# Product slabs of a deformable sampling summed by 32x32 tile matmuls, with GpSimd making three of the ten slabs

## The chip, the cores and the metric

The kernel runs on one core of a Trainium2 chip. The metric is the device time of one execution in microseconds; the median of three runs of the kernel before is 114.21 us (113.84 to 116.41). Engines are named as in the profile: PE is TensorE's matmul, PEld its weight load, DVE VectorE, ACT ScalarE, POOL GpSimd, SP SyncE with the DMA queue. A difference of about 2% is what is called a difference here.

## What is computed

A batch of four images, 64 channels, 16 by 16 points, goes through three layers: a deformable convolution block, a gated attention over the 256 tokens, and a mixture of eight experts of which two are used. The change lies in the first, in its sampling:

```python
def _bilinear_sample(img, grid):                 # img (8, 18, 18), grid (256, 9, 2)
    ...
    return gather(y0, x0) * w00 + gather(y0, x1) * w01 + gather(y1, x0) * w10 + gather(y1, x1) * w11

def _dcnv3_core(x, offset, mask):                # 8 groups of 8 channels, 9 points each
    ...
    sampled = jax.vmap(_bilinear_sample)(xin, sgf)
    m = mask.reshape(B, H * W, G, P).transpose(0, 2, 1, 3).reshape(B * G, 1, H * W, P)
    out = (sampled * m).sum(-1)
    ...
def _forward(...):
    h = gelu(conv1x1(x)); u = h; h = dwconv5(h)
    attn = dcn(h)                                # v = h @ inproj; offsets and softmax masks; _dcnv3_core; @ outproj
    attn = _conv1x1(attn, conv_w, conv_b)
    return _conv1x1(u * attn, proj2_w, proj2_b) + shortcut
```

## The kernel before

Every engine's program is written out by hand, in a fixed order, with semaphores between them. The four images are handled as two halves of two (`BL = 2`, called `bl` below and "first" and "second image"; each is really a pair, one on partitions 0 to 63, one on 64 to 127). Tokens lie on partitions in sampling, four x positions beside each other in the free dimension (`VW = 256` columns).

Sampling avoids the gather. As long as offsets stay under one point, the nine sampling points of a token touch a window of 5 by 5 pixels. `v_win` holds that window (five rows `dy`, loaded by 20 DMAs from `v_padded`). The 25 weights of the window are summed on PE: VectorE makes `ym` (hat functions in y times the softmax weights `prob`) and then three `terms` per image (`window_terms`, jx = 0 and 1 on VectorE, the third on GpSimd in `side_terms`), and `window_weights` on PE adds them through matmuls with the identity into PSUM (15 matmuls of up to 288 columns, 30 records: a float32 matmul is recorded as two). `products(bl, dy)` on VectorE then multiplies one row of the window, five taps of 256 columns, by its weights, which it reads from PSUM. These five slices of 256 columns are a product slab; there are five slabs per image. GpSimd's `merge` adds slices 3 and 4 into 0 and 1, and `window_sum` on PE adds the three slices that are left into `bank(bl, 2)`, with the full identity as weights. `MERGED = 5, 4` says how many slabs GpSimd merges; the last is merged by VectorE (`merge_last`).

`mask_sums` and `inverse_sums` make the softmax denominators on VectorE. `normalise` multiplies the sum by them, `to_channels` transposes on PE (8 matmuls of 64x64), `samples` copies on ScalarE, `project` and `close_l0` end the layer, with `shortcut` adding the layer's input in front. `flags` finds out whether some offset was too large; `over` on ScalarE sums the excess, GpSimd reads the flag and would compute the sampling slowly (with these inputs it doesn't) and then sets `slow_done`, for which `to_channels` waits. `keep_warm` issues matmuls on zeros while PE would be idle.

Matmul instructions of PE all carry the line of the helper `mm` (L1080).

## Time and profile before

| | |
|---|---|
| runs | 113.84, 114.21, 116.41 us |
| profiled execution, span | 114.8 us (114.82 in the trace) |
| granted TensorE clock, mean | 0.940 |
| instructions recorded | 1623, of them PE 569 matmuls and 573 weight loads |
| longest piece of the chain | PE, 57.38 to 68.97 us, 62 records |

The profile is that of one execution. Positions are microseconds from the span's start. In a timeline or in the chain, one line can stand for several instructions of the same kind that follow each other (x16): its time then reaches from the first's start to the last's end. Starts of a matmul are measured, its end is modelled, so a matmul's own time overlaps the next one's. An "idle before" in brackets names what ended the wait. The granted clock is a share of 2.4 GHz.

### The profile page before, as it was taken

How to read it: one execution, taken by the hardware profiler on the slowest of the kernel's cores; microseconds unless marked ns; L12 is line 12 of the kernel's file. 1: busy time of each engine (PE TensorE's matmuls, PEld its weight loads, DVE VectorE, ACT ScalarE, POOL GpSimd, SP SyncE). 2: the span in 40 equal slices, each digit the busy share in tenths (PEclk: the TensorE clock that was granted, in tenths of full speed). 3: DMA queues.
4: the chain of work that ended last, by engine and by line, in shares of the span. 5: the costliest groups of instructions: out<-in, count | busy, mean ns of one | idle time of the engine just before them, and what ended most of it. 6: DMA issues, size and time to landing. Idle time of an engine off the chain costs nothing.

```text
span 114.8 us, 1623 instructions
## 1 busy us (share of the span) xinstructions
PE 101.9 (89%) x569; PEld 71.4 (62%) x573; DVE 76.2 (66%) x172; ACT 48.0 (42%) x106; POOL 41.4 (36%) x51
## 2 busy tenths in 40 slices
PE   5999910999999899999799999899899899999990
PEld 1578800677745559899477786557696558864340
DVE  0489921799520699999999923657940836947751
ACT  2299200343980896100000023487833994964000
POOL 7137999089400072815799800000000006200000
PEclk9999998559965699999999999999999999999999
DMA  2995000000013662650000000000000000000002
GB/s 57 406 331 233 0 0 0 0 0 0 6 46 79 206 201 78 201 173 34 0 0 3 0 0 0 0 6 0 0 0 0 0 6 3 0 3 0 0 0 91
DMA packets 3225, 6.20 MB, mean 54 GB/s; under 512 B 528, under 2 KB 1296, under 8 KB 3216
## 3 DMA queue, kind: packets, MB, share of 16 engines
q1 hardware_dynamic: 2784, 4.64, 12.7%
q10 hardware_dynamic: 432, 1.46, 3.6%
q8 instruction: 4, 0.07, 0.2%
q14 instruction: 5, 0.04, 0.1%
HBM read 5.16 MB, written 0.93 MB: 53 GB/s over the span
## 4 chain that ended last, share of the span: by engine, by line
PE 56%; DVE 14%; ACT 10%; issue 10%; POOL 8%; DVEq 0%; ACTq 0%
PE ps L1080 55%; POOL prod L459 6%; DVE prod L861 3%; DVE ym L832 2%; DVE terms L841 2%; ACT prod L682 2%; ACT prod L602 1%; ACT L727 1%; ACT L595 1%; POOL prod L494 1%; DVE lmax L816 1%; DVE smax L908 1%; DVE psum_p L846 1%; ACT prod L615 1%; ACT upad L593 1%
## 5 line engine op out<-in xcount | busy, mean ns | idle before, releaser
L1080 PE MATMUL ps<-prod,wts 128*128 128x256 f32 (+1 forms) x122 | 28.8, 403 | 7.3 <-POOL prod L459 5.5
L1080 PEld LDWEIGHTS ps<-prod,wts 128*128 128x128 f32 (+1 forms) x122 | 17.6, 177 | 15.3 <-POOL prod L459 5.9
L1080 PE MATMUL ps<-terms,wts 128*128 128x256 f32 (+3 forms) x104 | 20.5, 350 | 0.0
L1080 PEld LDWEIGHTS ps<-terms,wts 128*128 128x128 f32 x104 | 16.9, 190 | 2.6 <-issue 0.4
L459 POOL TENSOR_TENSOR prod<-prod 128x256 f32<-128x256 f32 x10 | 12.8, 1313 | 5.7 <-ACT prod L602 5.7
L861 DVE TENSOR_TENSOR prod<-v_win,ps 128x1280 f32<-128x1280 f32 x10 | 14.3, 1462 | 0.0
L494 POOL TENSOR_TENSOR prod<-prod 128x512 f32<-128x512 f32 x9 | 11.5, 1273 | 5.3 <-DVE prod L861 4.9
L566 POOL TENSOR_TENSOR terms<-terms 128x256 f32<-128x256 f32 x2 | 1.4, 724 | 28.8 <-DVE terms L958 28.7
L669 ACT ACTIVATE samp_t<-ps 128x256 f32<-128x256 f32 x2 | 1.3, 640 | 23.3 <-PE ps L1080 23.3
L485 POOL TENSOR_TENSOR terms<-ym,hat 128x864 f32<-128x864 f32 x2 | 5.8, 2888 | 13.1 <-DVE ym L832 13.1
L1080 PE MATMUL ps<-idle 128*128 128x512 bf16 x27 | 8.7, 462 | 1.4 <-DVE idle L744 1.3
L1080 PE MATMUL ps<-upad,terms 128*128 128x256 f32 x36 | 8.1, 382 | 0.0
L762 DVE SCALAR_TENSOR_TENSOR acc<-upad,wts,acc 128x256 f32<-128x256 f32 x20 | 8.0, 476 | 0.0
L1080 PEld LDWEIGHTS ps<-upad,terms 128*128 128x128 f32 x36 | 6.8, 188 | 1.2
L1080 PEld LDWEIGHTS ps<-idle 128*128 128x128 bf16 x31 | 3.2, 109 | 6.4 <-issue 2.6
L1070 DVE TENSOR_TENSOR prod<-prod,ps 128x512 f32<-128x512 f32 x8 | 5.4, 687 | 2.3 <-PE ps L1080 2.3
L738 ACT ACTIVATE prod<-ps,wts 128x512 f32<-128x512 f32 x8 | 5.2, 687 | 2.0 <-PE ps L1080 2.0
L841 DVE TENSOR_TENSOR terms<-ym,hat 128x864 f32<-128x864 f32 x4 | 5.9, 1508 | 0.1
L1080 PE MATMUL ps<-wts,x 64*64 64x216 f32 x32 | 5.5, 509 | 0.5 <-issue 0.5
L602 ACT ACTIVATE prod<-hpad,wts 128x256 f32<-128x256 f32 x4 | 1.7, 497 | 10.0 <-DVE hpad L790 10.0
L1080 PE MATMUL ps<-hpad,cen 128*128 128x256 f32 x12 | 5.0, 602 | 0.0
L1080 PEld LDWEIGHTS ps<-hpad,cen 128*128 128x128 f32 x12 | 3.8, 328 | 1.3 <-issue 0.4
(165 smaller groups left out, 156.6 us busy)
## 6 DMA issues: line engine op xcount, KB each, us to landing
v_win<-v_padded SPq DMA_DIRECT2D x20, 128.0 KB, 2.8
wts<-in_w ACTq DMA_DIRECT2D x1, 984.0 KB, 8.5
wts<-in_w SPq DMA_DIRECT2D x1, 640.0 KB, 8.1
v_padded<-s_v SPq DMA_DIRECT2D x1, 400.0 KB, 8.1
wts<-in_w ACTq DMA_DIRECT2D x1, 280.0 KB, 4.1
x_in<-in_x SPq DMA_DIRECT2D x1, 256.0 KB, 3.2
v_padded<-v_tok SPq DMA_DIRECT2D x4, 64.0 KB, 2.0
out<-res SPq DMA_DIRECT2D x2, 128.0 KB, 1.7
```

Of the source, the lines that this page charges most:

```text
L459: g.tensor_tensor(part[:, bl, :], scaled[:, bl, 0, :] if k == 1 else part[:, bl, :], scaled[:, bl, k, :], ALU.add).then_inc(step[bl], 1)
L485: g.tensor_tensor(terms[:, bl, K3 - 1, :, :], ym[:, bl, :, :], hat[:, bl, K3 - 1, 0, :].unsqueeze(1).broadcast_to([P, K3, NPT * XG]), ALU. ...
L494: g.tensor_tensor(into, into, prod[:, bl, dy, 3:5, :], ALU.add).then_inc(merge_done, 1)
L602: a.activation(grid(scaled[:, bl, k, :]), padded[:, bl, y0:y0 + H, x0:x0 + W], ACT.Copy, scale=w(weights, first + k, first + k + 1)).then_ ...
L682: a.activation(pr[:, bl, bh * IT + it, :], bank(bl, bh)[:, it * HW:(it + 1) * HW], ACT.Exp, bias=nbias[:, bl, it, bh:bh + 1], accum_out=pr ...
L738: a.activation(h_act[:, bl, ep, :], hid_bank(bl, ep), ACT.Gelu, bias=w("b1", ep, ep + 1)).then_inc(gelu_done, 1)
L762: v.scalar_tensor_tensor(out=to, in0=src, scalar=w(weights, k, k + 1), in1=to, op0=ALU.mult, op1=ALU.add).then_inc(step[bl], 1)
L832: v.tensor_tensor(ym[:, bl, :, :], hat[:, bl, :, 1, :], prob[:, bl, :].unsqueeze(1).broadcast_to([P, K3, NPT * XG]), ALU.mult).then_inc(ym ...
L841: v.tensor_tensor(terms[:, bl, jx, :, :], ym[:, bl, :, :], hat[:, bl, jx, 0, :].unsqueeze(1).broadcast_to([P, K3, NPT * XG]), ALU.mult).th ...
L861: v.tensor_tensor(prod[:, bl, dy, :, :].rearrange("p d (x c) -> p d x c", c=GC), win, a5_rows(bl, dy, dy + 1)[:, 0].unsqueeze(3).broadcast ...
L1070: v.tensor_tensor(h_cmb[:, bl, ep % 2, :], h_act[:, bl, ep, :], bank(bl, 2), ALU.mult).then_inc(hcmb_done, 1)
L1080: return nc.tensor.matmul(out_, lhsT, rhs, start=start, stop=stop, skip_group_check=True)
```

## The change

- The three terms of an image are all made by VectorE, in the order jx = 1, 0, 2, image after image; GpSimd's `side_terms`, its merges, `merge_last` and the reduces `mask_sums` are gone.
- The softmax denominators are summed on PE: nine matmuls per image within `window_weights`, after the first of the three terms, into columns behind the weights (`mask_sum`). The reciprocal is taken image by image from PSUM.
- GpSimd makes three product slabs, (0, 4), (1, 3) and (1, 4). It cannot read PSUM, so ScalarE copies their window weights to SBUF (`copy_a5`).
- `window_sum` sums the 25 slices of 256 columns of an image by 100 matmuls of 32x32 (identity `ident4`): row group `r` of partitions goes to its own PSUM bank, slice `n` to the partitions of group `n % 4`. The four banks then hold four by four partial sums. ScalarE (for the second image ScalarE and VectorE) copies them to `by_slab`, and `sum_slabs` adds the four column groups by four matmuls that place every row group where it belongs. The banks 6 and 7 serve both images, so `window_sum(1, 0)` waits for the copies of the first.
- `shortcut` moves from in front of the second image's weights into `close_l0`; `to_channels` writes to bank 3, `t0` to bank 2. `sq`, `lnv`, `rstd`, `xn` become parts of one tensor `ln_room`, in which the copies also lie. `window_sum(0, 0)` waits for both images' flags.

```diff
-MERGED = 5, 4
+TILE = 32
+TG = P // TILE
+POOLED = (4,), (3, 4)
+        def slab_bank(bl, r):
+            return ps[:, ((2, 3, 6, 7), (0, 1, 6, 7))[bl][r], :]
 (GpSimd)
+            def products(bl, dy):
+                pool.wait_ge(v_windowed[bl], 16 * BH * K5)
+                pool.wait_ge(a5_copied, bl + 1)
...
+                g.tensor_tensor(prod[:, bl, dy, :, :].rearrange("p d (x c) -> p d x c", c=GC), win,
+                                weights.unsqueeze(3).broadcast_to([P, K5, XG, GC]),
+                                ALU.mult).then_inc(pool_prod_done, 1)
 (ScalarE)
+            def copy_a5(bl):
+                act.wait_ge(a5_done, bl + 1)
+            def copy_slabs(bl, half_):
+                act.wait_ge(slabs_done, bl + 1)
+                if bl:
+                    act.wait_ge(sum_done, bl)
 (TensorE)
+                    if jx == order[0]:
+                        for q in range(NPT):
+                            mm(mask_sum(bl), w("ident"), prob[:, bl, q * XG:(q + 1) * XG], False, False)
             def window_sum(bl, dy):
                 if dy == 0:
-                    pe.wait_ge(far_set, bl + 1)
+                    pe.wait_ge(ident4_set, 1)
+                    pe.wait_ge(far_set, BL)
+                    if bl:
+                        pe.wait_ge(prod_done, K5 - len(POOLED[0]))
+                        pe.wait_ge(slabs_act, 2)
...
+                for dx in range(K5):
+                    n = dy * K5 + dx
+                    o0, o1 = row_group(n % TG)
+                    for r in range(TG):
+                        p0, p1_ = row_group(r)
+                        last = mm(slab_bank(bl, r)[o0:o1, 0:VW], ident4[p0:p1_, :],
+                                  prod[p0:p1_, bl, dy, dx, :], n < TG, n >= K5 * K5 - TG)
+            def sum_slabs(bl):
+                pe.wait_ge(slabs_act, (2, 3)[bl])
+                if bl:
+                    pe.wait_ge(slabs_dve, 1)
+                for r in range(TG):
+                    o0, o1 = row_group(r)
+                    last = mm(bank(bl, 2)[o0:o1, 0:VW], ident4[:, :], by_slab[:, r, :])
+                last.then_inc(sum_done, 1)
             def close_l0(bl):
+                pe.wait_ge(xb_ready, 1)
+                mm(bank(bl, 3)[:, 0:HW], w("center"), xb[:, bl, :], True, False)
```

Where instructions stand now. On PE, before, from the last two terms of the first image's weights (jx = 0) to the second image's first term and then from the sums on (`terms,wts` are window weights, `over_sum` the flags, `xb` the shortcut):

```order
L1080 MATMUL ps<-terms,wts 128x3x96
L1080 MATMUL ps<-terms,wts 128x2x96
L1080 MATMUL ps<-terms,wts 128x96 x2
L1080 MATMUL ps<-terms,wts 128x2x96
L1080 MATMUL ps<-wts,over_sum 1x1 x2
L1080 MATMUL ps<-xb,wts 128x256 x2
L1080 MATMUL ps<-terms,wts 128x3x96
```

The same place with the change:

```order
L1112 MATMUL ps<-prob,wts 128x32 x9
L1112 MATMUL ps<-terms,wts 128x3x96
L1112 MATMUL ps<-terms,wts 128x2x96
L1112 MATMUL ps<-terms,wts 128x96 x2
L1112 MATMUL ps<-terms,wts 128x2x96
```

The nine `prob` matmuls stand behind the first term of each image, and the shortcut is no longer between the flags and the second image's weights.

PE from the second image's weights to the last close, before:

```order
L1080 MATMUL ps<-prod,wts 128x256 x24
L1080 MATMUL ps<-wts,samp 64x64 x8
L1080 MATMUL ps<-prod,wts 128x256 x6
L1080 MATMUL ps<-samp_t,w_oc 128x256
L1080 MATMUL ps<-wts,samp 64x64 x8
L1080 MATMUL ps<-zu,w2c 128x256
L1080 MATMUL ps<-zu,wts 128x256
L1080 MATMUL ps<-samp_t,w_oc 128x256
```

And with the change:

```order
L1112 MATMUL ps<-prod,ident 32x256 x120
L1112 MATMUL ps<-ln_room,ident 32x256 x4
L1112 MATMUL ps<-prod,ident 32x256 x20
L1112 MATMUL ps<-wts,samp 64x64 x8
L1112 MATMUL ps<-prod,ident 32x256 x20
L1112 MATMUL ps<-samp_t,w_oc 128x256
L1112 MATMUL ps<-prod,ident 32x256 x40
L1112 MATMUL ps<-xb,wts 128x256
L1112 MATMUL ps<-zu,w2c 128x256
L1112 MATMUL ps<-zu,wts 128x256
L1112 MATMUL ps<-ln_room,ident 32x256 x4
L1112 MATMUL ps<-wts,samp 64x64 x8
```

30 matmuls became 200 and eight more; `to_channels(0)`, `project(0)` and `close_l0(0)` lie between the second image's slabs.

ScalarE with the change, behind the exponential of the second image, waits named (L684 is `over`, L691 `copy_a5`, L699 `copy_slabs`, L705 `samples`):

```order
L684 ACTIVATE s_pos,over_sum<-o_abs,wts 128x576 [waits abs_done]
L691 ACTIVATE ln_room<-ps 128x160 [waits a5_done]
L684 ACTIVATE s_pos,over_sum<-o_abs,wts 128x576 [waits abs_done]
L691 ACTIVATE ln_room<-ps 128x320 [waits a5_done]
L699 ACTIVATE ln_room<-ps 128x512 [waits slabs_done] x2
L705 ACTIVATE samp_t<-ps 128x4x64 [waits sT_done]
L699 ACTIVATE ln_room<-ps 128x512 [waits sum_done,slabs_done]
```

Before, the two `over` instructions followed each other directly, and then came the two `samples`. The second `over`, for which the flags on PE wait, is now behind a copy that waits for the first image's weights.

## Rows read from the trace of the kernel before

**Rows 1.** The page: busy time of each engine, share of the span, instructions.
```profile
PE 101.9 (89%) x569; PEld 71.4 (62%) x573; DVE 76.2 (66%) x172; ACT 48.0 (42%) x106; POOL 41.4 (36%) x51
```
**Rows 2.** The chain of work in order of time: start us, us, what.
```profile
57.38 11.59 PE ps L1080 x62
...
68.99 0.43 DVE samp L879
```
**Rows 3.** Timeline of PE, weights to slabs: start us, us, engine, line, operation, tiles.
```profile
42.56 4.91 PE L1080 MATMUL ps<-terms,wts 128*128 128x288 f32 x30
47.40 0.24 PE L1080 MATMUL ps<-wts,over_sum 128*1 128x1 f32 x4
47.57 1.13 PE L1080 MATMUL ps<-xb,wts 128*128 128x256 f32 x4
48.53 4.91 PE L1080 MATMUL ps<-terms,wts 128*128 128x288 f32 x30
53.28 1.89 PE L1080 MATMUL ps<-prod,wts 128*128 128x256 f32 x8
```
**Rows 4.** Timeline of DVE products; then two groups of GpSimd adds (busy us, mean ns).
```profile
55.96 7.05 DVE L861 TENSOR_TENSOR prod<-v_win,ps 128x1280 f32<-128x1280 f32 x5
...
L494 POOL TENSOR_TENSOR prod<-prod 128x512 f32<-128x512 f32 x9 | 11.5, 1273 | 5.3 <-DVE prod L861 4.9
...
L566 POOL TENSOR_TENSOR terms<-terms 128x256 f32<-128x256 f32 x2 | 1.4, 724 | 28.8 <-DVE terms L958 28.7
```
**Rows 5.** Timeline of softmax and terms: DVE, GpSimd, and ScalarE's `over`.
```profile
38.13 0.66 DVE L816 TENSOR_REDUCE lmax<-lg 128x32 f32<-128x288 f32 x1 [4.47 <-ACT lg L637]
...
39.88 1.06 DVE L832 TENSOR_TENSOR ym<-hat,prob 128x864 f32<-128x864 f32 x1 [0.24 <-ACT prob L655]
40.97 1.06 DVE L841 TENSOR_TENSOR terms<-ym,hat 128x864 f32<-128x864 f32 x1
...
44.62 0.76 ACT L663 ACTIVATE s_pos<-o_abs,wts 128x576 f32<-128x576 f32 x1
45.28 0.19 ACT L663 ACTIVATION_READ_ACCUMULATOR s_pos<-o_abs,wts 128x1 f32 x1
...
46.34 3.85 DVE L841 TENSOR_TENSOR terms<-ym,hat 128x864 f32<-128x864 f32 x2
46.38 2.88 POOL L485 TENSOR_TENSOR terms<-ym,hat 128x864 f32<-128x864 f32 x1 [2.47 <-DVE ym L832]
```
**Rows 6.** Timeline of PE's weight loads at the router (16 columns each).
```profile
94.83 0.52 PEld L1080 LDWEIGHTS ps<-wts,terms 128*128 128x128 f32 x4 [0.26 <-DVE terms L958]
```
**Rows 7.** Groups of ScalarE's copies out of PSUM: busy us, mean ns.
```profile
L688 ACT ACTIVATE prod<-ps 128x512 f32<-128x512 f32 x2 | 1.2, 597 | 1.4 <-PE ps L1080 1.4
L676 ACT ACTIVATE terms<-ps 128x256 f32<-128x256 f32 x2 | 0.8, 390 | 0.0
```
**Rows 8.** Timeline of 64x64 matmuls; the second row is 74.77 to 74.81 alone.
```profile
74.78 1.09 PE L1080 MATMUL ps<-terms 64*64 64x256 f32 x16
...
74.78 0.45 PE L1080 MATMUL ps<-terms 64*64 64x256 f32 x4
...
65.48 0.54 PEld L1080 LDWEIGHTS ps<-wts,samp 64*64 64x64 f32 x16 [0.33 <-issue]
```
**Rows 9.** Timeline of the tail, ScalarE and PE.
```profile
68.79 0.59 PE L1080 MATMUL ps<-samp_t,w_oc 128*128 128x256 f32 x2
...
70.19 0.63 ACT L669 ACTIVATE samp_t<-ps 128x256 f32<-128x256 f32 x1 [3.33 <-PE ps L1080]
...
71.05 0.59 PE L1080 MATMUL ps<-samp_t,w_oc 128*128 128x256 f32 x2
...
73.08 0.59 PE L1080 MATMUL ps<-zu,wts 128*128 128x256 f32 x2
```
**Rows 10.** Stretches: us, busy PE, PEld, DVE, ACT, POOL, clock, DMA share, GB/s.
```profile
31.00:33.00 2.00, 2.00 (x27) 1.55 (x25) 0.42 (x1) 1.97 (x4) 0.00 (x0) 0.92 0.00 0
33.00:39.00 6.00, 5.53 (x29) 2.68 (x28) 1.26 (x3) 2.31 (x5) 0.00 (x0) 0.50 0.41 118
```

More of the change, by code:

```diff
@@ L118, in conv_attn_moe @@
         acc3 = sb("acc3", [P, BL, HW])
-        sq = sb("sq", [P, BL, HW])
-        lnv = sb("lnv", [P, BL, HW])
-        rstd = sb("rstd", [P, BL, HW])
-        xn = sb("xn", [P, BL, HW])
+        ln_room = sb("ln_room", [P, 4 * BL, HW])
+        sq, lnv, rstd, xn = (ln_room[:, i * BL:(i + 1) * BL, :] for i in range(4))
         x1 = sb("x1", [P, BL, HW])
@@ L479, in _ @@
                     left = b2_rest[:, i, :]
-            def side_terms(bl):
-                pool.wait_ge(ym_done, bl + 1)
-                pool.wait_ge(hats_done, 2 * bl + 2)
-                g.tensor_tensor(terms[:, bl, K3 - 1, :, :], ym[:, bl, :, :],
-                                hat[:, bl, K3 - 1, 0, :].unsqueeze(1).broadcast_to([P, K3, NPT * XG]),
-                                ALU.mult).then_inc(side_terms_done, 1)
-            def merge(bl):
-                for dy in range(MERGED[bl]):
-                    pool.wait_ge(prod_done, K5 * bl + dy + 1)
-                    into = prod[:, bl, dy, 0:2, :]
-                    g.tensor_tensor(into, into, prod[:, bl, dy, 3:5, :], ALU.add).then_inc(merge_done, 1)
+            def products(bl, dy):
+                pool.wait_ge(v_windowed[bl], 16 * BH * K5)
+                pool.wait_ge(a5_copied, bl + 1)
+                row = v_win[:, bl, dy, 0:VW]
+                win = bass.AP(row.tensor, row.offset, [list(row.ap[0]), [C, K5], [GC, XG], [1, GC]])
+                weights = a5_rows_sb[:, bl, dy - AR, :].rearrange("p (d x) -> p d x", d=K5)
+                g.tensor_tensor(prod[:, bl, dy, :, :].rearrange("p d (x c) -> p d x c", c=GC), win,
+                                weights.unsqueeze(3).broadcast_to([P, K5, XG, GC]),
+                                ALU.mult).then_inc(pool_prod_done, 1)
+            for dy in POOLED[0]:
+                products(0, dy)
+            products(1, POOLED[1][0])
             for bl in range(BL):
-                side_terms(bl)
-            for bl in range(BL):
-                merge(bl)
+                if bl:
+                    for dy in POOLED[1][1:]:
+                        products(1, dy)
                 pool.wait_ge(far_set, bl + 1)
@@ L706, in _ @@
             over(0)
+            copy_a5(0)
             over(1)
+            copy_a5(1)
+            copy_slabs(0, 1)
+            copy_slabs(0, 0)
             samples(0)
+            copy_slabs(1, 0)
             samples(1)
@@ L958, in normed3 @@
                 v.tensor_tensor(x2[:, bl, :], bank(bl, 0)[:, 0:HW], rstd3[:, bl, :], ALU.mult).then_inc(x2_done, 1)
-            softmax(0)
-            masked_hats(0)
-            window_terms(0, 1)
-            softmax(1)
-            window_terms(0, 0)
-            masked_hats(1)
-            window_terms(1, 1)
-            window_terms(1, 0)
-            mask_sums(0)
-            products(0, 0)
-            flags(0)
-            mask_sums(1)
-            products(0, 1)
-            inverse_sums()
-            products(0, 2)
+            for bl in range(BL):
+                softmax(bl)
+                masked_hats(bl)
+                for jx in (1, 0, 2):
+                    window_terms(bl, jx)
+            flags(0)
+            inverse_sums(0)
+            products(0, 0)
             flags(1)
-            products(0, 3)
-            products(0, 4)
+            for dy in range(1, K5):
+                if dy not in POOLED[0]:
+                    products(0, dy)
+            inverse_sums(1)
             products(1, 0)
             products(1, 1)
+            normalise(0)
             products(1, 2)
-            normalise(0)
-            products(1, 3)
-            products(1, 4)
-            merge_last()
+            gate_u(0)
+            copy_slabs(1, 1)
             normalise(1)
-            gate_u(0)
             gate_u(1)
@@ L1303, in _ @@
             flags(1)
-            for bl in range(BL):
-                shortcut(bl)
             window_weights(1)
@@ L1309, in _ @@
             window_sum(1, 0)
+            sum_slabs(0)
             window_sum(1, 1)
+            to_channels(0)
             window_sum(1, 2)
-            to_channels(0)
+            project(0)
             window_sum(1, 3)
             window_sum(1, 4)
-            project(0)
+            close_l0(0)
+            sum_slabs(1)
             to_channels(1)
-            close_l0(0)
             project(1)
```

82 lines of the change are left out of this document (44 added, 38 removed).

## Prediction

> **What bounds the kernel now.** I read the page's summary first [rows 1]: PE is busy 89% of the span, VectorE 66%. The chain in order of time [rows 2] says where this change acts: 62 PE records from 57.38 to 68.97 are its longest piece, and the second image's `normalise` at 68.99 ends it. The timeline of PE [rows 3] gives the positions that all sums below start from. The first image's window weights (30 records) start at 42.56, the next work at 47.40, so they take 4.84; the second image's start at 48.53, and the first slab is fed at 53.28. After that PE has 60 full-array records of 256 columns, 0.213 apart ((1.89 - 0.4) / 7 [rows 3]), 12.8 us, and reaches `project(0)` at 68.79 [rows 9], because VectorE hands over a product every 1.41 us and GpSimd merges one in 1.27 [rows 4]. So two things alternate as the bound: PE up to 53.3, then the trio of VectorE, GpSimd and PE at nearly equal pace. The change gives the second stretch a new shape and makes the first one longer.
>
> **The front: window weights.** All terms now come from VectorE: three of 1.06 behind each `ym`. From the first at 40.97 that puts the end of the first image's third at 44.15; from softmax's start to `ym` 1.75 (38.13 to 39.88), `ym` 1.06 and three more terms: 50.1 [rows 5]. VectorE took the second image's two terms in 3.85 instead of 2.1, because GpSimd's 2.88 instruction lay beside them [rows 5]; without that neighbour the third term costs VectorE nothing: 50.1 is also when it was free before. PE needs the terms later than they come.
> New on PE are the mask sums, nine matmuls (18 records) per image of 32 columns with the full 128-column `ident` as weights. The nearest row is the router, 16 columns behind full weights: four weight loads in 0.52, each lasting 0.19, so (0.52 - 0.19) / 3 = 0.11 a record [rows 6]. 18 x 0.11 = 1.98 an image. First image: 42.56 + 4.84 + 1.98 = 49.4.
> Then ScalarE stands in the way: `over(1)` is now behind `copy_a5(0)`, which waits for those weights. From PE being free to ScalarE's start 0.2 (68.79 to the `normalise` at 68.99 [rows 2, 9]); copy of 160 columns about 0.3 (256 take 0.39 [rows 7]); `over(1)` 0.85 (44.62 to 45.47 [rows 5]). So PE's `flags(1)` waits until 50.8, and behind it in PE's queue are all second weights: 50.9 + 4.84 + 1.98 = **57.7**. Before, that was 53.2. PE idles 1.4 there, and the first slab is summed 4.5 us later, although VectorE has made its four products by 56.3 (from 50.5, behind flag and reciprocal, 1.41 each) and GpSimd its one.
>
> **The slabs.** A slab is now 20 matmuls of 32x32, 40 records of 256 columns. No row shows a 32x32 tile. What rows show is 64x64: 16 records of 256 columns in 1.09, four of them beginning within 0.04 [rows 8]; one after another they would need 3.4. Four tiles really run at once. With sixteen, 40 x 0.213 / 16 = 0.53 a slab; that is the lower bound. Upper bound: the eight 64x64 matmuls of 64 columns, 16 loads in 0.54 of which the last lasts 0.13, 0.41 / 15 = 0.027, at 40 records 1.1 a slab; were no tile to run beside another, 8.5, which the same rows exclude. I call the cost s and take s = 0.60: the four-tile row is the nearest, and it loses only at its end.
> The Trainium skill, "TensorE: Matmul & The Clock Gate", section "Measured speedup vs the span model", gives 10.6 times for sixteen tiles, not 16. By it, s = 20 x 0.427 / 10.6 = 0.81, and the sum below would be 1.9 us longer. Its number is for one isolated pack; it is the first rival below.
>
> **The sum from 57.7.** Five slabs of the first image in one go (5s). Then `window_sum(1, 0)` must wait for ScalarE to empty the same banks: 0.2 + two copies of 512 columns at 0.60 [rows 7] = 1.4. One slab (s). `sum_slabs(0)`, eight records on four column tiles, 0.45, semaphore 0.2. `normalise` 0.42, and only behind it product (1, 2), 1.47 with its gap. Slab (1, 1) and `to_channels(0)` hide under these. Slab (1, 2) (s), `project(0)` 0.43, two slabs (2s); `close_l0(0)`, now with the shortcut, three matmuls 1.3, which hides the two copies of the last slabs (0.2 + 0.6); `sum_slabs(1)` 0.45, 0.2. Constants 6.35, so `normalise(1)` starts at 57.7 + 6.35 + 9s = 64.05 + 9s, which is 9s - 4.94 later than before. At 0.60 that is 69.45; before it was 68.99 [rows 2]: **+0.46**.
> GpSimd: three products. From 256 to 512 elements its add goes from 0.72 to 1.27, and the 864 ones, without the wait for VectorE's 1.06, last 49.26 - 47.40 = 1.86 [rows 4, 5]; on that line 1280 elements cost about 2.7, at worst 2.888 x 1280 / 864 = 4.3. The second image's two start at 58.3 and end at 63.7 (at worst 66.9). PE asks for the last one s + 1.95 before the end of the sum, at 62.1 + 8s = 66.9. Cost nothing, even at worst. GpSimd's far test (`slow_done`) comes behind the first of them, at 61.1, before `to_channels(0)` asks at 63.8. Before, products on VectorE beside merges on GpSimd lasted the usual 1.41 [rows 4], so these two forms don't block each other.
> VectorE loses two reduces, a merge and three products, and gains two terms and a copy; idle from 56.3 to 58.3, it is no longer a bound, so this is worth nothing by itself.
> The tail: `close_l0(0)` no longer stands before `project(1)`, but ScalarE's `samp_t` copy is in front of it anyway (70.82 against 71.05 [rows 9]); the shortcut, once in front of the weights (0.96 between 47.57 and 48.53, counted above), now adds 0.43 to the stretch `project(1)`, variance, two idle matmuls, `close_l0(1)`. Start of the last `proj2`: 69.45 + 0.43 + 0.7 + 0.7 + 0.1 = 71.4 for `project(1)`, five matmuls of 0.43 behind it, 73.5; before 73.08. So the tail gives back nothing and adds nothing: total **+0.5**. Profiled span 114.82, so 115.3; the median of the runs shown, 114.21, is 0.6 under the profiled execution, so **114.7 us**.
>
> **Rivals.** A difference of about 2% (2.3 us) is what a measurement of this kernel can tell from no change.
> *Each pack pays its end* (14%). The 16 records of the four-tile row took 1.09, where four rounds of 0.213 are 0.85; if every slab pays that 0.24, s = 0.77 and the time is 114.2 + 9 x 0.77 - 4.94 = 116.2. For it: every slab but the first image's starts after a wait. Against: five slabs run back to back.
> *The small matmuls are limited by issue* (15%), the slower side. A slab has 80 instructions where it had 12. If a pair never takes less than the 0.027 of the short 64x64 row, s = 1.1 and the time is 114.2 + 9.9 - 4.9 = 119.2. It decides from s = 0.80 upward. Against it: in that row the columns themselves (64 on two tiles) fill the time, and in the other one eight instructions begin within 0.04 [rows 8]. The Trainium skill, "Runtime: NRT & Kernel Launch", section "Instruction fetch mechanics", speaks of about 20 sequencer cycles an instruction; by it s would be 1.33 and the time some 2 us above this rival. The 0.04 speaks against that, but only for a short run of instructions.
> *The clock falls* (12%). The granted clock was 0.50, its lower level of 1.2 GHz, from 33 to 39 after a stretch of small 64x64 matmuls in which PE counted as busy nearly all the time [rows 10]. The same after these sparse stretches: six microseconds at half clock, somewhat over half of them PE-bound, +3.5: 118.2.
> *Weights that stay* (7%), the faster side: if the repeated `ident` loads cost 0.03 instead of 0.11, 36 x 0.08 = 2.9 comes off the front: 111.8. The router row and the 96-column pieces in the 4.84 speak against it.
> That the work isn't moved at all can't be: order and data are fixed in the program.
>
> **Numbers.** Forecast 50%, others as above, 2% for what I haven't seen. Within 2%: the forecast and half of the first rival, 0.57. Slower: 0.15 + 0.12 + 0.07 + 0.02 = 0.36. Faster 0.07. The range leaves out most of the faster case and the top of the issue case: 112.8 to 118.9. The forecast's own range is 113.9 to 115.6 (s from 0.53 to 0.65, 0.4 either way for copies and semaphores).
>
> **What would show it.** Second weights end on PE near 57.7 with a gap of 1.4 before them; mask sums 2.0 an image; five slabs in 2.7 to 3.2; a gap of 1.4 behind them; `normalise(1)` at 69.5; clock at its upper level throughout; GpSimd products 2.7. I am wrong if five slabs take over 4, or if the weights come before 56.

## The result, and the profile after

The changed kernel takes 119.09 us (median of four runs, 118.03 to 121.41), the kernel before, measured beside it, 115.29 us (113.84 to 116.41): a ratio of 1.041 with a 95% interval of 1.028 to 1.055. It is slower; the forecast was 114.7 with a range up to 118.9.

Executions of every kernel here come in a faster and a slower kind, so ratios and their intervals compare the faster ones alone, while medians and the lowest and highest time take all. The first window weights start near 40 us in some profiles and near 43 us in others, in which the granted clock stands at a half for longer before them. So dates are compared from the start of the first window weights, which I call W. The profiled execution of the changed kernel has W at 43.04; before it was 42.56 [rows 3], so 0.48 of every later date is not the change's.

The page of the changed kernel, to be read against [rows 1, 4]: the summary, and three groups of section 5 (line, engine, operation, tiles, count, then busy us and mean ns of one, then idle before).

```profile
PE 103.4 (87%) x961; PEld 71.3 (60%) x965; DVE 70.4 (59%) x171; ACT 50.3 (42%) x111; POOL 31.6 (26%) x43
...
L510 POOL TENSOR_TENSOR prod<-v_win,ln_room 128x1280 f32<-128x1280 f32 x3 | 7.2, 2417 | 25.8 <-ACT ln_room L691 25.8
...
L1112 PE MATMUL ps<-prod,ident 32*32 32x256 f32 x400 | 10.0, 385 | 1.5 <-ACT ln_room L699 1.4
```

VectorE lost 5.8 us of work and GpSimd 9.8; PE gained 1.5 although its matmuls became small. So the engines that shared the second stretch are relieved, and PE alone paces it. The mean of 385 ns for a tile's record of 256 columns is not the price of one, since up to sixteen lie over each other; what they cost together has to be read from the timeline.

The timeline of PE in the changed kernel, from the first window weights to the second image's turn to channels (start us, us, engine, line, operation, tiles, records, and in brackets the idle time before with what ended it), against [rows 3, 9]:

```profile
43.04 1.75 PE L1112 MATMUL ps<-terms,wts 128*128 128x288 f32 x10
44.62 2.09 PE L1112 MATMUL ps<-prob,wts 128*128 128x32 f32 x18
...
51.10 0.19 PE L1112 MATMUL ps<-wts,over_sum 128*1 128x1 f32 x2 [1.03 <-ACT s_pos L684]
...
58.18 4.08 PE L1112 MATMUL ps<-prod,ident 32*32 32x256 f32 x200
63.64 1.35 PE L1112 MATMUL ps<-prod,ident 32*32 32x256 f32 x40 [1.38 <-ACT ln_room L699]
64.91 0.64 PE L1112 MATMUL ps<-ln_room,ident 128*32 128x256 f32 x8
65.48 1.29 PE L1112 MATMUL ps<-prod,ident 32*32 32x256 f32 x40
66.71 0.68 PE L1112 MATMUL ps<-wts,samp 64*64 64x64 f32 x16
67.49 1.29 PE L1112 MATMUL ps<-prod,ident 32*32 32x256 f32 x40
68.72 0.70 PE L1112 MATMUL ps<-samp_t,w_oc 128*128 128x256 f32 x2
69.35 1.99 PE L1112 MATMUL ps<-prod,ident 32*32 32x256 f32 x80
71.27 0.70 PE L1112 MATMUL ps<-xb,wts 128*128 128x256 f32 x2
```

The chain of work of the same stretch (start us, us, what), where [rows 2] had one piece of 62 PE records:

```profile
51.10 11.17 PE ps L1112 x226
62.27 0.02 issue
62.30 1.09 ACT ln_room L699 x2
63.39 0.24 issue
63.64 1.96 PE ps L1112 x47
65.60 0.02 issue
65.62 0.07 DVE samp L919
65.69 0.28 issue
65.96 1.49 DVE prod L907
67.45 0.04 issue
67.49 5.95 PE ps L1112 x129
73.44 0.02 issue
73.47 0.44 DVE samp L919
```

`normalise(1)` starts at 73.47, 30.43 after W; before it was 68.99 - 42.56 = 26.43. The 4.0 us between them are the whole loss: from there to the end of the span it is 45.8 or 45.9 in both (119.34 - 73.47, 114.82 - 68.99). They split at the first slab on PE: it starts 15.14 after W (58.18 - 43.04) where it was 10.72 (53.28 - 42.56 [rows 3]), 4.4 later, and from there to `normalise(1)` it is 15.29 where it was 15.71, 0.4 less. So the new summing is no slower than the old one. It was to win back 4.0 of what the front costs (15.71 - 11.75 by the forecast) and won back 0.4. The chain is PE nearly throughout; the only other links are two copies of ScalarE and one `normalise` with a product behind it.

### The profile page after: what moved, and what is told of

The parts are those of the page before. It is cut to its first block, busy times and chain, and to the rows that moved or that the text cites. A ratio compares the mean times of both kernels' runs of the same rounds, so it can differ in the third digit from the quotient of the medians.

```text
span 119.3 us, 2412 instructions
## 1 busy us (share of the span) xinstructions
PE 103.4 (87%) x961; PEld 71.3 (60%) x965; DVE 70.4 (59%) x171; ACT 50.3 (42%) x111; POOL 31.6 (26%) x43
## 4 chain that ended last, share of the span: by engine, by line
PE 69%; ACT 11%; POOL 6%; DVE 6%; issue 5%; ACTq 0%; DVEq 0%
PE ps L1112 69%; POOL prod L481 6%; ACT prod L718 2%; DVE prod L907 1%; ACT prod L623 1%; ACT L768 1%; ACT L616 1%; DVE smax L948 1%; ACT ln_room L699 1%; ACT upad L614 1%; ACT terms L643 1%; ACT terms L641 1%; ACT prod L636 1%; ACT s_pos L684 1%; ACT samp_t L705 1%
## 5 line engine op out<-in xcount | busy, mean ns | idle before, releaser
L1112 PE MATMUL ps<-terms,wts 128*128 128x256 f32 (+3 forms) x104 | 21.1, 352 | 0.0
L1112 PE MATMUL ps<-prod,wts 128*64 128x256 f32 (+1 forms) x62 | 14.3, 410 | 6.6 <-POOL prod L481 5.5
L510 POOL TENSOR_TENSOR prod<-v_win,ln_room 128x1280 f32<-128x1280 f32 x3 | 7.2, 2417 | 25.8 <-ACT ln_room L691 25.8
L1112 PEld LDWEIGHTS ps<-prod,wts 128*64 128x64 f32 (+1 forms) x62 | 7.0, 165 | 11.1 <-POOL prod L481 5.9
L1112 PE MATMUL ps<-prod,ident 32*32 32x256 f32 x400 | 10.0, 385 | 1.5 <-ACT ln_room L699 1.4
L907 DVE TENSOR_TENSOR prod<-v_win,ps 128x1280 f32<-128x1280 f32 x7 | 10.0, 1458 | 0.0
L1112 PEld LDWEIGHTS ps<-prod,ident 32*32 32x32 f32 x400 | 5.9, 103 | 4.7 <-issue 3.0
L691 ACT ACTIVATE ln_room<-ps 128x160 f32<-128x160 f32 (+1 forms) x2 | 0.7, 372 | 10.6 <-PE ps L1112 10.6
```

The source lines that it names most:

```text
L510: g.tensor_tensor(prod[:, bl, dy, :, :].rearrange("p d (x c) -> p d x c", c=GC), win, weights.unsqueeze(3).broadcast_to([P, K5, XG, GC]), ...
L907: v.tensor_tensor(prod[:, bl, dy, :, :].rearrange("p d (x c) -> p d x c", c=GC), win, a5_rows(bl, dy, dy + 1)[:, 0].unsqueeze(3).broadcast ...
L1112: return nc.tensor.matmul(out_, lhsT, rhs, start=start, stop=stop, skip_group_check=True)
```

## Experiments

Two kinds of question were open: why nine slabs cost 8.4 us on this path where 5.4 had been forecast, and what the other parts of the change (mask sums on PE, the order of `over`, GpSimd's slabs) are worth. In what follows a *turn* is four slices of 256 columns: four row groups times four column groups, each of the sixteen tiles used once, 16 matmuls, 32 records. By columns alone a turn lasts 2 x 0.213 = 0.427 us.

### Half the columns

```diff
-                        last = mm(slab_bank(bl, r)[o0:o1, 0:VW], ident4[p0:p1_, :],
-                                  prod[p0:p1_, bl, dy, dx, :], ...)
+                    wide = VW if n < TG else VW // 2
+                        last = mm(slab_bank(bl, r)[o0:o1, 0:wide], ident4[p0:p1_, :],
+                                  prod[p0:p1_, bl, dy, dx, 0:wide], ...)
```

> The changed kernel, but all slab matmuls except the first sixteen of each image stream 128 of the 256 columns (half of the sampling's sum is left out in those columns). It tells apart what sets the pace of the 200 records of the first image, which began within 3.70 us (58.18 to 61.88). Theory 1, issue: a pair of weight load and matmul cannot be fed faster than one per about 17 ns, so the 200 records still take 3.3 to 3.7 us. Theory 2, columns and tiles: the pace is that of the columns, 0.213 for 256, so the 168 shortened records run at about half and the stretch falls to 2.0 to 2.2 us. The single slabs of the second image (1.23 us each until PE is free): theory 1 about 1.2, theory 2 about 0.8.

Timeline of PE in this kernel:

```profile
54.75 3.02 PE L1112 MATMUL ps<-prod,ident 32*32 32x256 f32 x200
...
60.80 0.87 PE L1112 MATMUL ps<-prod,ident 32*32 32x128 f32 x40
61.60 0.68 PE L1112 MATMUL ps<-wts,samp 64*64 64x64 f32 x16
```

The first copy of the partial sums starts at 57.80, so the burst of five slabs takes 3.05 where it took 4.12 (62.30 - 58.18). A slab by itself went from 1.23 to 0.80 (61.60 - 60.80), two turns of 0.213 less. The burst, with 21 of its 25 slices halved, lost 1.07, five times 0.213; six of its seven turns hold halved slices. So columns count nearly in full, and neither theory holds alone: pure issue would have left the burst nearly as it was, pure columns would have made it 2.1.

The starts of single records, read in the trace one by one, say what lies above the columns. Behind the first turn of the changed kernel's burst, a group of 34 records starts every 0.645 us (at 58.83, 59.47, 60.12, 60.77, 61.41), with one pause of 0.16 in each. With half the columns the group comes every 0.43 with a pause of 0.04. A tile's two passes are 0.427 and 0.213, so both lie 0.22 above them. For a turn of 32 records that makes 0.61 and 0.41, some 0.18 above the columns in either case.

### Four slices of the second image's slabs

```diff
-                for dx in range(K5):
-                    n = dy * K5 + dx
+                taps_used = (K5, K5 - 1)[bl]
+                for dx in range(taps_used):
+                    n = dy * taps_used + dx
```

The sum of image 1 leaves out one of five slices of each slab here.

> The changed kernel with the fifth slice (dx = 4) of each of the second image's slabs left out, so that a slab standing alone is 16 matmuls, one for every tile. Theory A, second turn: five slices on four column groups need some tiles twice, 2 x 0.427, and then PE waits for the end of the last, 0.38, before it changes its tile shape; 1.24 in all. Without the fifth slice it is 0.43 + 0.38 = 0.81, so slab (1, 2) falls from 1.23 to 0.8 and slab (1, 0) from 1.27 to about 0.85. Theory B, issue: the cost follows the number of instructions, 1.23 x 4/5 = 0.98.

Timeline of PE in this kernel, three slabs that stand alone and the last two in one run, with what follows each:

```profile
60.51 0.96 PE L1112 MATMUL ps<-prod,ident 32*32 32x256 f32 x32 [1.38 <-ACT ln_room L699]
61.41 0.64 PE L1112 MATMUL ps<-ln_room,ident 128*32 128x256 f32 x8
61.98 0.73 PE L1112 MATMUL ps<-prod,ident 32*32 32x256 f32 x32
62.64 0.68 PE L1112 MATMUL ps<-wts,samp 64*64 64x64 f32 x16
63.99 0.73 PE L1112 MATMUL ps<-prod,ident 32*32 32x256 f32 x32 [0.67 <-DVE prod L907]
64.64 0.70 PE L1112 MATMUL ps<-samp_t,w_oc 128*128 128x256 f32 x2
65.27 1.50 PE L1112 MATMUL ps<-prod,ident 32*32 32x256 f32 x64
66.70 0.70 PE L1112 MATMUL ps<-xb,wts 128*128 128x256 f32 x2
```

Slabs (1, 1) and (1, 2) of four slices take 0.66 (62.64 - 61.98) and 0.65, one of five took 1.23. The first slab, which starts behind a wait for ScalarE, takes 0.90 where it took 1.27. So the fifth slice costs 0.4 to 0.6, as much as up to four others: it opens a second turn. Theory B's 0.98 is out; theory A had the turn right and its 0.8 somewhat too high. A second turn that is filled costs more still, as the last two slabs show (66.70 - 65.27). All runs of slices that were measured with 256 columns, from the first record's start to what follows on PE (for the 25, to the first copy):

| slices in a run | turns | their columns, us | measured, us |
|---|---|---|---|
| 4 | 1 | 0.43 | 0.65, 0.66, behind a wait 0.90 |
| 5 | 2 | 0.85 | 1.23, behind a wait 1.27 |
| 8 | 2 | 0.85 | 1.43 |
| 10 | 3 | 1.28 | 1.92 |
| 20 | 5 | 2.13 | 3.58, 4.06, 4.26 (three kernels further down) |
| 25 | 7 | 2.99 | 4.12 |

Whole turns of columns are a lower bound that every run keeps; 0.2 to 0.6 us come on top in the short ones, 1.1 in the burst, 1.5 and more at 20 slices. The simplest rule, 0.65 for the first turn and 0.58 for each one more, fits 4, 5 and 25 slices, and is short by 0.20 at 8, by 0.11 at 10 and by 0.6 or more at 20.

### Another order of the same matmuls

```diff
-                for dx in range(K5):
-                    for r in range(TG):
+                for n0 in range(0, K5 * K5, TG):
+                    for r in range(TG):
+                        for n in range(n0, min(n0 + TG, K5 * K5)):
```

> The burst of image 0 in another order: of four products at a time the four of one row group one after the other, then those of the next row group, where the changed kernel has the four row groups of one product and then the next product. The same 100 matmuls on the same tiles. Theory A (each turn of all sixteen tiles costs its columns, 0.427 us, and about 0.16 us for issuing its 32 pairs of records, in whatever order): the 200 records to the first copy of partial sums take 4.1 us again. Theory B (the order makes the tiles wait for one another): 3.4 us, or well over 4.5 where this order is the worse one.

The burst starts at 58.77, the first copy at 63.21: 4.44, 0.32 more than in the changed kernel. The pitch is the same (34 records every 0.65, with the same pause of 0.16). What is longer is the end: the last 31 records take 0.79 from the first start to the last, where it was 0.48. In this order the last slice needs row group 3 again only four matmuls after its last use; whether that is what delays it was not tested. Theory A holds for the pitch; my 4.1 missed the end.

### Tiles of 64x64, and no tiles

```diff
-TILE = 32
+TILE = 64
```

with `w("ident2")` for `ident4`, and without `copy_slabs(0, 1)` and `copy_slabs(1, 1)`, as two banks do.

> The slabs are summed with 64x64 tiles (two row groups, two column groups): 50 matmuls of an image in place of 100, two banks in place of four, one copy in place of two, and the same tile shape as the turns to channels. Column theory (a tile takes 0.427 us, four run at once): the burst of 25 products takes 13 turns of 0.427, 5.5 us, and a slab alone 3 turns, 1.3 us; the first slab of image 1 no longer waits for copies. The second normalise comes about 0.4 us earlier than in the changed kernel, 118.7 us. Issue theory (18.5 ns for each of the 100 records is all that counts): the burst takes 1.9 us and a slab alone 0.4 plus its end, the normalise comes 5 us earlier, 114 us.

Timeline of PE in the kernel with 64x64 tiles, the burst with the slab behind it, and `sum_slabs(0)`:

```profile
54.83 7.12 PE L1108 MATMUL ps<-prod,wts 64*64 64x256 f32 x120
61.88 0.65 PE L1108 MATMUL ps<-ln_room,wts 128*64 128x256 f32 x4
```

The copy starts at 60.71, 5.88 after the burst did: 13 turns of two slices, 13 x 0.427 = 5.55, and 0.33 for the end. With eight records in a turn there is no extra at all (four start together every 0.216), with 32 there is 0.18. Column theory right, issue theory refuted for this size. Whether the extra comes with the number of records or of tiles stays open, as this run changes both. The sum of the gains was wrong, though: `normalise(1)` comes 31.42 after W (71.04 - 39.62), 1.0 later than in the changed kernel where I had it 0.4 earlier. I had counted the wait for the copies as saved, 1.34, but not that a slab of five slices then takes three turns each time, 1.51 and 2.39 for two where the small tiles take 1.29 and 1.99. The time is 120.4 us (four executions of 118.9 to 122.8; the changed kernel's 118.0 to 121.4), which tells no difference.

The other end is the full array:

```diff
+                    last = mm(bank(bl, 2)[:, 0:VW], w("ident"), prod[:, bl, dy, dx, :], n == 0, n == K5 * K5 - 1)
```

> The 50 matmuls of the product slabs are 128x128 ones with the identity (0.427 us each for 256 columns), summed in one bank, with no 32x32 tiles, no copies of partial sums and no final sums. Price by columns: the 25 of image 0 take 10.7 us where the tiles took 4.1 and their copies and sum 3.3 more, so the first normalise comes 3.4 us later; the second 7 to 8 us later, about 126.5 us. Had the tiles brought nothing over the full array in this place, the time would stay near 119.

Timeline of PE in the kernel without tiles:

```profile
57.90 15.27 PE L1108 MATMUL ps<-prod,wts 128*128 128x256 f32 x70
```

70 records at 0.217; `normalise(1)` 38.07 after W (80.93 - 42.86), 7.6 later than with tiles, 129.6 us. The tiles do shorten the summing. Against the merging of the kernel before, where VectorE and GpSimd took work off PE, they come out about even: 15.29 from the first slab to `normalise(1)`, 15.71 before.

### The mask sums back on VectorE

```diff
-                    if jx == order[0]:
-                        for q in range(NPT):
-                            mm(mask_sum(bl), w("ident"), prob[:, bl, q * XG:(q + 1) * XG], False, False)
+            def mask_sums(bl):
+                v.tensor_reduce(psum_p[:, bl, :], prob[:, bl, :].rearrange("p (q x) -> p x q", q=NPT), AX_X, ...)
```

> The mask sums go back from TensorE (two runs of nine matmuls, 18 records each, 2.09 us a run) to two reduces on VectorE, placed behind the first and the seventh VectorE product. Theory (the front is paced by TensorE): the weights of image 1 end 3.9 us earlier, the burst of five slabs starts there and still takes 4.1 us, the second normalise comes 3.5 to 4.0 us earlier, about 115.4 us. Rival (VectorE takes over the pace, since its fourth product of image 0 would end near 56.5 and be waited for): the burst stretches to 5 us and the gain is 2 to 2.5 us, about 116.8 us.

(The diff leaves out that the reciprocals read the new sums.) Neither number was met: `normalise(1)` 29.22 after W (68.74 - 39.52), 1.2 earlier than in the changed kernel. Timelines of this kernel, first VectorE's terms of the two images (the last row is the second of the three, by itself), then GpSimd's first product, then PE's last two terms of image 1 and the burst:

```profile
38.32 3.00 DVE L886 TENSOR_TENSOR terms<-ym,hat 128x864 f32<-128x864 f32 x3
...
44.06 5.22 DVE L886 TENSOR_TENSOR terms<-ym,hat 128x864 f32<-128x864 f32 x3
...
45.04 3.27 DVE L886 TENSOR_TENSOR terms<-ym,hat 128x864 f32<-128x864 f32 x1
```

```profile
44.99 2.41 POOL L512 TENSOR_TENSOR prod<-v_win,ln_room 128x1280 f32<-128x1280 f32 x1 [14.94 <-ACT ln_room L693]
```

```profile
48.37 3.43 PE L1119 MATMUL ps<-terms,wts 128*128 128x288 f32 x20 [0.75 <-DVE terms L886]
51.73 5.87 PE L1119 MATMUL ps<-prod,ident 32*32 32x256 f32 x200
```

The three terms of image 1 took 5.22 where those of image 0 took 3.00. With the mask sums gone from PE, the first weights end 2 us earlier after W, ScalarE's copy too, and GpSimd starts its product at 44.99, in the middle of VectorE's terms: 2.2 us more, all of it in the one term that started 0.05 after the product: it lasted 3.27 and ended 0.9 after the product did (48.31, 47.40). The other two took the usual 1.05. PE then waits for a term, and its burst stretches to 5.87 because VectorE's products are late. In the changed kernel GpSimd started at 50.44, behind the terms, and they took 3.00; there the mask sums on PE, 1.93 an image, had kept the two apart.

### GpSimd's first product held back

```diff
                 pool.wait_ge(v_windowed[bl], 16 * BH * K5)
+                pool.wait_ge(terms_done, K3 * BL)
```

> Mask sums on VectorE as in the run before it, and one wait more: GpSimd's first product starts only when VectorE's last terms are made. Theory (VectorE and GpSimd slow each other when both read and write SBUF alone): the three terms of image 1 take 3.0 us again where they took 5.2 beside GpSimd's product, all of VectorE behind them is 2.2 us earlier, the second normalise comes 27.0 us after the first window weights in place of 29.2, about 115.5 us. Rival (the terms were slow for another reason, TensorE reading them or the clock): they stay at 5.2 us, GpSimd's product is 2 us later for nothing, and the time is 117.5 us or more.

Timelines of this kernel, VectorE's terms of image 1 and then GpSimd's first product:

```profile
43.87 3.00 DVE L887 TENSOR_TENSOR terms<-ym,hat 128x864 f32<-128x864 f32 x3
```

```profile
47.00 2.41 POOL L513 TENSOR_TENSOR prod<-v_win,ln_room 128x1280 f32<-128x1280 f32 x1 [16.99 <-DVE terms L887]
```

Three terms 3.00, and `normalise(1)` 27.01 after W (66.34 - 39.33), as the theory had it. 114.57 us, ratio to the kernel before 1.001 (0.996 to 1.007). GpSimd's neighbourhood was the cause. It hits only some forms: beside the same instruction of GpSimd, VectorE's products of image 0 took 4.26 for three, the usual 1.42 each. They read one operand from PSUM, the terms read both from SBUF; no run changes that alone. This is what the Trainium skill, "SBUF — State Buffer", section "SBUF: two separate sides", says of a VectorE instruction with two SBUF inputs beside a GpSimd one that reads SBUF: one of them waits for the whole of the other. The trace agrees: the term that met the product got done only behind it, at a loss of 2.2 us against a product of 2.41.

### The overflow measure first

```diff
-            copy_a5(0)
             over(1)
+            copy_a5(0)
```

> The changed kernel with one swap on ScalarE: over(1) before copy_a5(0). The flags of the second image no longer wait for the copy, so PE's gap of 1.03 us before them goes, and the second image's weights start 1.1 us earlier. If PE is the bound from there to normalise(1), as every theory of mine has it, the time falls by 1.0 to 1.1 us (ratio to the kernel before about 1.03 instead of 1.04). If the sampling is bound by something else (products on GpSimd or VectorE), it falls by less than 0.5.

Timeline of PE in this kernel, flags and the second image's weights:

```profile
49.87 0.24 PE L1112 MATMUL ps<-wts,over_sum 128*1 128x1 f32 x4
50.04 1.85 PE L1112 MATMUL ps<-terms,wts 128*128 128x288 f32 x10
```

The gap of 1.03 is gone, `normalise(1)` comes 29.26 after W (72.28 - 43.02), 1.2 earlier, and the span of 118.2 is 1.1 under that of the changed kernel. The timed ratio, 1.040 (1.025 to 1.055), is too wide to show a gain of 1%; the claim rests on the trace.

### The last four slabs in one run

```diff
-            window_sum(1, 1)
-            to_channels(0)
-            window_sum(1, 2)
-            project(0)
-            window_sum(1, 3)
-            window_sum(1, 4)
-            close_l0(0)
-            sum_slabs(1)
+            for dy in range(1, K5):
+                window_sum(1, dy)
+            to_channels(0)
+            sum_slabs(1)
+            project(0)
```

and `products(1, 2)` ahead of `normalise(0)`, with `gate_u(0)` behind `normalise(1)` on VectorE and `copy_slabs(1, 0)` ahead of `samples(0)` on ScalarE.

> The changed kernel with another order: slabs (1, 1) to (1, 4) follow each other on PE, with to_channels(0) behind them and project(0) and close_l0(0) behind sum_slabs(1); VectorE makes product (1, 2) before normalise(0). Theory A (a slab alone costs 1.2 to 1.3, in a row 0.75): the four slabs take 3.0 to 3.2 from 65.4, normalise(1) starts near 70.0 instead of 73.47, close_l0(0) is now in the way of project(1), and the time falls by 2.5 to 3 us, ratio to the kernel before about 1.015. Theory B (the front decides, the slabs' form does not matter): normalise(1) moves by less than 1 and the time stays within 1 us of the changed kernel's.

Timeline of PE in this kernel, the four slabs and the turn to channels:

```profile
65.67 4.13 PE L1112 MATMUL ps<-prod,ident 32*32 32x256 f32 x160
69.73 0.68 PE L1112 MATMUL ps<-wts,samp 64*64 64x64 f32 x16
```

`normalise(1)` 28.09 after W (71.37 - 43.28), 2.3 earlier, where I had expected 3.5. And 0.9 of it is given back behind, 46.7 to the end of the span instead of 45.8, where `project(0)`, `close_l0(0)` and `gate_u(0)` now come later. Ratio 1.020 (1.006 to 1.033). The four slabs took 4.06 where I had 3.0 to 3.2. One pause lies inside the run: 0.51 pass between two record starts at 67.34 and 67.86, 0.14 of it idle, and the profile names no releaser. It is no wait for data, as VectorE's and GpSimd's products were all made by 63.9. The pause and the rest of the difference stay unexplained.

### The parts together

On TensorE and ScalarE alone (the two orders above, and the first slab of image 1 waiting for the one copy that frees the banks it writes):

```diff
-                        pe.wait_ge(slabs_act, 2)
+                        pe.wait_ge(slabs_act, 1)
```

> The changed kernel with its mask sums left on TensorE, the overflow measure of image 1 first (worth 1.2 us at the second normalise), the four last slabs in one run (worth 1.7 us there), and the first slab of image 1 waiting for one copy instead of two (0.65 us if nothing else is late). Theory (the three are worth what they are worth alone, since VectorE's products have been ready for long): the second normalise 26.9 us after the first window weights in place of 30.4, about 115.6 us. Rival (VectorE's products of image 1 or GpSimd's are late next): 0.7 to 1.2 us of that is lost, about 116.5 us.

26.70 after W (67.65 - 40.95; 26.9 expected), 115.76 us, ratio 1.008 (1.002 to 1.014). The three parts add up as expected. The four slabs, 4.26 here, have a pause again, of 0.35 idle, with all products made by 60.5.

And with the mask sums on VectorE behind its fifth and seventh products and GpSimd's first product held back as well:

```diff
 (VectorE, in products)
                 if dy == 0:
+                    dve.wait_ge(a5_copied, bl + 1)
 (VectorE)
+            products(1, 0)
+            mask_sums(0)
+            inverse_sums(0)
+            products(1, 1)
+            products(1, 2)
+            normalise(0)
+            mask_sums(1)
+            inverse_sums(1)
 (GpSimd)
+                pool.wait_ge(terms_done, K3 * BL)
```

The first product of an image now waits itself for ScalarE's copy out of the same bank, as the reciprocal that had this wait no longer does. An earlier form, with the sums behind the first product and behind `normalise(0)`, without this wait and without the one for GpSimd, gave no time.

> Mask sums on VectorE behind its fifth and seventh products, the overflow measure of image 1 ahead of the copy of weights' rows, GpSimd's first product held back until the last terms are made, the four last slabs of image 1 in one run, and the first slab of image 1 waiting for one of the two copies instead of both. Counted from the start of the first window weights, the second normalise was at 30.4 us in the changed kernel and at 29.2 with the mask sums alone moved. Theory (VectorE paces the front once the mask sums are off TensorE; GpSimd beside it is what stretched its terms): terms end at 7.1, four products at 12.8, the burst 1.1 us later at 13.9, first slab of image 1 from 14.6, second normalise 10 us behind it at 24.6 to 25.5, about 114 us. Rival (the terms stay at 5.2 us for three without GpSimd beside them): 2.2 us later, about 116.2 us.

Timeline of PE in this kernel, from the burst on:

```profile
53.64 4.64 PE L1121 MATMUL ps<-prod,ident 32*32 32x256 f32 x200
59.16 1.28 PE L1121 MATMUL ps<-prod,ident 32*32 32x256 f32 x40 [0.89 <-ACT ln_room L702]
...
60.95 3.65 PE L1121 MATMUL ps<-prod,ident 32*32 32x256 f32 x160
```

The burst starts 10.1 after W where it was 15.1, and 0.55 longer than before, as its last VectorE product comes late; `normalise(1)` 22.65 after W (66.18 - 43.53), better than the 24.6 I had expected although the first slab of image 1 came at 15.6 and not at 14.6, because the four slabs need 3.6 and the copies are no longer all waited for (I had allowed 10 us from the first slab of image 1 on; it is 7.0). 0.9 is given back behind it, as in the two other kernels with this order. 112.59 us, seven runs, against 115.11 for the kernel before: ratio 0.977 (0.966 to 0.989). This version is faster than the changed kernel, and than the kernel before by 1 to 3%: a gain clear of noise, but not surely one of 2%.

Dates of the profiled executions, medians of the timed ones beside the median of the kernel before that was run with them, and the ratio where there is one:

| kernel | burst after W | `normalise(1)` after W | rest of the span | time, us | before, us | ratio |
|---|---|---|---|---|---|---|
| before | 10.72 | 26.43 | 45.8 | | 115.29 | |
| changed | 15.14 | 30.43 | 45.9 | 119.09 | 115.29 | 1.041 |
| `over` first | 13.97 | 29.26 | 45.9 | 119.85 | 116.73 | 1.040 |
| slabs in one run | 15.14 | 28.09 | 46.7 | 117.33 | 116.73 | 1.020 |
| mask sums on VectorE | 12.21 | 29.22 | 45.9 | 117.87 | 115.29 | |
| the same, GpSimd held back | 11.19 | 27.01 | 45.9 | 114.57 | 115.11 | 1.001 |
| both orders, one copy | 14.04 | 26.70 | 46.7 | 115.76 | 115.11 | 1.008 |
| all together | 10.11 | 22.65 | 46.7 | 112.59 | 115.11 | 0.977 |

## Why the prediction was wrong, by its steps

**What bounds the kernel** held: the change acts in the stretch up to `normalise(1)`, and PE alone paces it afterwards.

**The front** held to a tenth in its end: second weights ended at 58.18 - 0.48 = 57.7, as forecast. Mask sums 1.93 an image (46.55 - 44.62; forecast 1.98), the gap before `flags(1)` 1.03 with 0.19 of the first flag in front of it (forecast 1.4), VectorE's terms 3.00 for three. That the front costs 4.5 us was forecast, too, and 4.4 measured is more than the whole loss of 4.0. The forecast let the slabs pay it back.

**The slabs**: the failed step. "I call the cost s and take s = 0.60". Nine slabs were to cost 5.4; measured in the same places: five in 4.0 (4.12 less a semaphore of 0.1), then 1.27, 1.23 and 1.92 for two, together 8.4, a mean of 0.94. The mechanism, tiles that run at once and PE as the bound, was right; the size of this term was not. Two things were missing. First, whole turns: 0.53 divided a slab's 40 records by sixteen as if they packed without remainder. Five slices on four column groups need two turns, 0.85 by columns; the last two slabs need three, 1.28, and the burst seven, 2.99. That is 5.98 for the nine, so the lower bound of 0.53 was too low for all of them, and s = 0.60 was used up by columns in the burst alone. Second, and larger, what comes on top of the columns: 8.4 - 6.0 = 2.4 us, of which 1.0 in the burst (0.18 for each full turn of sixteen tiles), 0.4 in each of the two lone slabs and 0.6 in the last two. The four-tile row of [rows 8] could show only its end of 0.24: with four tiles in use the turns have no extra, as the run with 64x64 tiles has shown at length. By the prediction's own sign, "five slabs take over 4", it was wrong here: 4.12 to the first copy.

**The sum**, term by term, measured minus forecast:

| term | forecast | measured | |
|---|---|---|---|
| burst, copies of four banks | 4.40 | 5.46 (58.18 to 63.64) | +1.06 |
| slab (1, 0), `sum_slabs(0)` | 1.25 | 1.98 (to 65.62) | +0.73 |
| `normalise(0)`, product (1, 2) | 1.89 | 1.87 (to 67.49) | -0.02 |
| slab (1, 2) | 0.60 | 1.23 (to 68.72) | +0.63 |
| `project(0)` | 0.43 | 0.63 (to 69.35) | +0.20 |
| two slabs | 1.20 | 1.92 (to 71.27) | +0.72 |
| `close_l0(0)`, `sum_slabs(1)` | 1.95 | 2.20 (to 73.47) | +0.25 |

Together +3.57, against 73.47 - 0.48 - 69.45 = 3.54 (the terms above make 69.42, as the prediction's constants are 6.32 and not 6.35). 3.0 of it are slabs. The rest is 0.2 for each piece of full-array matmuls between tiles, two changes of shape (`project(0)` lasts 0.63 from start to start where a matmul in a row of its like takes 0.43; the three of `close_l0(0)` take 1.49), and 0.06 each for the copies and the two `sum_slabs`, less 0.02 at `normalise(0)`.

**GpSimd** held: 2.42 a product (2.7 forecast), nobody waited for it, and products on VectorE beside it were not slowed. The other half of that step, that the terms lose their delay without a GpSimd neighbour [rows 5], held too (3.00 for three). Not seen was that GpSimd's new products could become such a neighbour again; in the changed kernel only the dates kept them apart.

**The tail** held: 45.8 or 45.9 from `normalise(1)` to the end in both kernels.

**The clock** held. The windows of the changed kernel (length, busy time of PE, PEld, DVE, ACT and POOL, then the granted clock, and last DMA share and GB/s) show it at its upper level of 2.4 GHz, 1.00, throughout:

```profile
57.00:62.00 5.00, 5.00 (x209) 3.83 (x207) 3.10 (x3) 0.44 (x1) 3.13 (x3) 1.00 0.02 5
62.00:68.00 6.00, 4.52 (x155) 2.37 (x138) 1.82 (x2) 1.65 (x3) 1.71 (x2) 1.00 0.01 3
68.00:74.00 6.00, 5.45 (x123) 2.96 (x106) 1.60 (x3) 0.69 (x2) 0.00 (x0) 1.00 0.02 4
```

**The rivals.** *Each pack pays its end* had the right idea at a third of its size: an end for each pack, but 0.77 a slab where a lone one costs 1.23. *Limited by issue* named a time, 119.2, that the measurement hit, yet not by its mechanism: it wanted 0.027 for every pair at any width, and halving the columns took 1.07 us off the burst. Its s of 1.1 is near the lone slab and far from 0.82 in the burst, so that it met the time is luck. The estimate of 0.81, worked out in the prediction from the Trainium skill, "TensorE: Matmul & The Clock Gate", "Measured speedup vs the span model", fits the burst (4.12 / 5 = 0.82) and would have put the time at 116.6; for lone slabs it is too low, 1.23 each. By the prediction's estimate from the about 20 cycles an instruction of the Trainium skill, "Runtime: NRT & Kernel Launch", "Instruction fetch mechanics", the burst would need 5 x 1.33 = 6.7 us; it took 4.1, so the trace does not bear it out here. *The clock falls* did not come about in this stretch, as the windows show, and neither did *weights that stay*: 18 records of mask sums took 1.93, 0.107 each.

## What to carry to other kernels

Price work on TensorE's small tiles in whole turns, not by dividing records by tiles: count how often the tile that is used most is used between two waits, and multiply by its columns. That is a lower bound (6.0 for the nine slabs here, 8.4 measured); with all sixteen tiles in use a turn in a long run took 0.61 us instead of 0.43, and a piece of another shape between tiles 0.2 more. Group slices so that they fill their turns, and let as few waits as can be cut a run. When work moves between VectorE and GpSimd, look not only at what each costs but at which instructions with all operands in SBUF will now meet: taking 3.9 us off PE gave 1.2 until one wait kept the two engines apart, and then 3.4. And count what a change puts in front: 4.4 us there outweighed the 0.4 that the slabs gave back. In the version that is faster in the end the first slab starts 10.1 after W, 0.6 earlier than in the kernel before.

## What was not expected of the hardware

- In a long run, a turn of sixteen 32x32 tiles costs 0.61 us for 0.427 of columns, and with 128 columns 0.41 for 0.213; with four 64x64 tiles nothing comes on top (13 turns in 5.88). In the trace, 34 records start every 0.645 us, in two different orders of the matmuls. What inside TensorE makes it was not settled. A fixed pause for issuing does not describe it, as the pause shrinks from 0.16 to 0.04 when the columns are halved.
- Three terms on VectorE took 5.22 us beside a GpSimd product of 2.41, 3.00 otherwise; one of them, started 0.05 behind the product, took all of the 2.2.
- The same run of 160 tile records took 3.58, 4.06 and 4.26 us in three kernels, the two longer ones with one pause each (0.14 and 0.35 idle) that no releaser ends and no product explains. It stays open.
